# A two-layer megakernel: the last stores and last operand parts of three stages issued in the stage that follows

## The reference, cut to what matters

```python
x = L0_attn_in_features                      # [4, 1024, 128] f32
xn = _layernorm(x)
s = _L0_attn_ref(xn, ...)                    # RoPE, causal softmax attention, 16 heads of 8
g = _silu(_L0_ffn_ref(xn, ...))              # 128 -> 512 -> 128, gelu, with a low-rank term
x = x + s * g
xn = _layernorm(x)
s = _L1_attn_ref(xn, ...)                    # retention: qk * decay mask, / clip(sum|qk|, 1, 5e4), @ v, RMS norm, * silu gate
g = _silu(_L1_ffn_ref(xn, ...))              # mixture of 8 experts, top 2, capacity 614 of each
x = x + s * g
```

## Time and profile before

| | |
|---|---|
| three timed runs | 1003.27, 1003.89, 1009.45 us, median 1003.89 |
| the profiled execution | 1005.31 us |
| span of its instructions | 1003.5 us |
| mean granted TensorE clock | 0.936 of full speed |
| barrier into the attention | 118.7 us from the span's start |
| barrier into the layer change | 543.1 us |
| barrier into the retention | 651.1 us |
| barrier into the experts | 886.3 us |

### The profile page before, as it was taken

How to read it: one execution, slowest core, us unless ns; L and a number is a source line. 1 busy time by engine, 2 the same in 40 slices (tenths; PEclk the granted TensorE clock), 3 DMA queues, 4 the chain that set the end, 5 groups by cost and what they waited for, 6 DMA issues and landing times. The chain is left out here.

```text
span 1003.5 us, 25274 instructions
## 1 busy us (share of the span) xinstructions
PE 868.0 (86%) x9413; PEld 464.8 (46%) x9414; DVE 799.3 (80%) x1691; ACT 726.1 (72%) x1493; POOL 290.2 (29%) x331
## 2 busy tenths in 40 slices
PE   3999899999999999999898799788899999979960
PEld 3676544333433333333333677533444444458850
DVE  6665499999999999999831565289999999938895
ACT  2666408888888888888775455388999999948851
POOL 4875311111111000000003666600344443005560
PEclk9999859999999999999989789969999999979995
DMA  5579861644444354430005678597364542546637
GB/s 167 201 266 331 290 152 42 206 100 102 107 102 117 85 126 78 80 71 21 13 13 139 211 241 231 172 221 142 70 119 94 115 90 54 136 143 192 209 116 253
DMA packets 119385, 140.92 MB, mean 140 GB/s; under 512 B 20109, under 2 KB 82138, under 8 KB 118624
## 3 DMA queue, kind: packets, MB, share of 16 engines
q1 hardware_dynamic: 113888, 127.45, 46.6%
q0 software_dynamic: 5376, 11.85, 4.1%
HBM read 77.63 MB, written 63.25 MB: 140 GB/s over the span
## 5 line engine op out<-in xcount | busy, mean ns | idle before, releaser
L868 ACT ACTIVATE probsB<-psB 128x512 f32<-128x512 f32 (+2 forms) x640 | 310.2, 565 | 86.3 <-PE psB L942 59.3
L779 DVE TENSOR_REDUCE mxB<-psB 128x1 f32<-128x512 f32 (+2 forms) x448 | 256.9, 647 | 9.8 <-PE psB L906 8.3
L935 PE MATMUL psB<-q_groups,k_groups 64*128 64x512 bf16 (+3 forms) x768 | 206.4, 332 | 15.1 <-DVE mxB L779 8.3
L906 PE MATMUL psB<-k_groups,q_groups 64*128 64x512 bf16 (+3 forms) x768 | 216.9, 343 | 2.9 <-PEq L306 1.7
L973 PE MATMUL psB<-probsB,vB 128*32 128x512 f32 (+3 forms) x1536 | 165.3, 502 | 0.7 <-ACT probsB L868 0.5
L1751 ACT ACTIVATE psD<-psD 128x896 f32<-128x896 f32 (+2 forms) x192 | 153.4, 799 | 14.6 <-PE psD L1805 14.4
L935 PEld LDWEIGHTS psB<-q_groups,k_groups 64*128 64x128 bf16 x768 | 67.5, 94 | 160.4 <-ACT probsB L868 140.9
L1682 DVE TENSOR_REDUCE sumsD<-psD 128x1 f32<-128x128 f32 (+3 forms) x256 | 113.8, 487 | 13.2 <-PE psD L1828 11.0
L1805 PE MATMUL psD<-k_groups,q_groups 64*128 64x512 bf16 (+3 forms) x384 | 102.7, 341 | 17.6 <-PEq L1063 6.5
L913 PE MATMUL psB<-hideB,chooseB 64*128 64x128 bf16 (+1 forms) x1024 | 115.1, 210 | 0.0
L779 DVE TENSOR_REDUCE mx2B<-psB 128x1 f32<-128x384 f32 (+2 forms) x192 | 104.8, 598 | 8.5 <-PE psB L913 6.4
(11 more groups left out here) (226 smaller groups left out, 1495.0 us busy)
## 6 DMA issues: line engine op xcount, KB each, us to landing
v<-vaugA SPq DMA_DIRECT2D x4, 2048.0 KB, 8.9
vB<-v SPq DMA_DIRECT2D x16, 512.0 KB
q_groups<-q SPq DMA_DIRECT2D x32, 200.0 KB
k_groups<-k SPq DMA_DIRECT2D x32, 200.0 KB
back<-emptyB POOLq DMA_DIRECT2D x16, 256.0 KB, 3.8
o<-outB SPq DMA_DIRECT2D x128, 32.0 KB, 1.8
xD<-xn SPq DMA_DIRECT2D x8, 512.0 KB, 7.1
q<-hiA SPq DMA_DIRECT2D x12, 256.0 KB, 6.6
```

What stands on the lines that cost most here:

```text
L779: nc.vector.tensor_reduce(dst, src, AX.X, ALU.max).then_inc(max_read, 1)
L868: nc.scalar.activation(probs[:, n % DEEP, 0:w], st[n % BANKS][:, 0:w], ACT.Exp, scale=DH ** -0.5).then_inc(exp_done, 1)
L906: ins = nc.tensor.matmul(bank[:, to:to + w], q[half[r], s, hq // 2, t * P:t * P + P], k[half[r], s, hq // 2, HALF * c:HALF * c + w], start ...
L935: ins = nc.tensor.matmul(bank[:, to:to + w], k[half[r], s, hq // 2, jt * P:jt * P + P], q[half[r], s, hq // 2, i0:i0 + w], start=True, sto ...
```

## The change

`LastParts` and `LastBanks` are buffers that outlive one stage; `last_out` lies with the buffers of the layer change. At the three stage ends:

1. Attention to layer change: the 4 stores of the last half group (x = 15, c = 1) go to the start of the layer change on SP. ACT of the layer change no longer waits for them (`wait_heads_but_last`), SP still does, before it loads the last denominators.
2. Layer change to retention: of the last batch the `mid` stores (2 DMAs) and the `lo` part (4 POOL subtractions of 128x512 and 2 DMAs) go to the retention. There POOL forms `lo` with 2 subtractions of 128x1024 right at the start. SP issues the `mid` stores behind the 24 group loads, and the `lo` stores between the expert inputs of batches 1 and 2; batches 2 and 3 are loaded over the same memory, so SP waits there until all four stores have landed.
3. Retention to experts: the last group's `o` (4 DMAs) and `sums` stores and the last `diag` store go to the start of the expert stage on SP, ahead of its loads.

The labels of the expert rows are written by 8 POOL copies of 128x16 and not by 2 of 128x64. DVE and POOL get a wait for the stores of `project_and_ffn` in the attention, since other memory now lies under their buffers; the maxima `mx`, `mx2` move to `Groups`, and the final `x1` and `res` take the memory of `outD` and of `LastParts`.

```diff
+def store_heads(sp, A, x, c, held, stored):
+    b, s = divmod(x, QUADS)
+    for hq in range(4):
+        sp.dma_start(A["o0"][b, 4 * s + hq, :, c * HALF:(c + 1) * HALF], held[VW * hq:VW * hq + 2 * DH, :]).then_inc(stored[c], 16)
+class LastParts:
...
+    def form_lo(self, nc):
+        for j in range(2):
+            ins = nc.gpsimd.tensor_tensor(self.lo[:, j, :], self.rest[:, j, :], self.mid[:, j, :], ALU.subtract)
+        ins.then_inc(self.ready, 1)
+    def store(self, sp, A, name, part):
+        for layer, parts in (("q1", Q_PARTS), ("k1", K_PARTS)):
+            r, j = DH * parts[name], 0 if layer == "q1" else 1
+            sp.dma_start(A[layer][B - 1, :, r:r + DH, :], part[:, j, :]).then_inc(self.stored, 16)
...
+    def wait_heads_but_last(self, engine):
+        for c in range(2):
+            engine.wait_ge(self.heads_stored[c], HEAD_STORES * (B * QUADS - c))
...
             engine.wait_ge(self.x1_stored, 32 * B + 1)
         for i in range(2):
-            engine.wait_ge(self.second_stored[i], 16 * SECOND_STORES * (B // 2) + 1)
+            engine.wait_ge(self.second_stored[i], 16 * (SECOND_STORES * (B // 2) - 4 * i) + 1)
...
-                    store(x, 1)
+                    if x + 1 < NQ:
+                        store(x, 1)
...
                     if n == AHEAD:
+                        kept_until.wait_rows(dve)
...
+                kept_until.wait_rows(pool)
                 for x in range(NQ):
                     split_maxima(x)
...
+                store_heads(sp, A, B * QUADS - 1, 1, second.last_out, kept_until.heads_stored)
                 kept_until.wait_heads(sp)
...
-                        sp.wait_ge(g["mid_ready"], count[i]["mid_ready"])
-                        store_parts(i, "mid", mid)
-                        sp.wait_ge(g["lo_ready"], count[i]["lo_ready"])
-                        store_parts(i, "lo", lo)
+                        if not last or i == 0:
+                            sp.wait_ge(g["mid_ready"], count[i]["mid_ready"])
+                            store_parts(i, "mid", mid)
+                            sp.wait_ge(g["lo_ready"], count[i]["lo_ready"])
+                            store_parts(i, "lo", lo)
...
-                        for half, c in enumerate(halves):
+                        for half, c in enumerate(halves if not last or i == 0 else ()):
                             pool.wait_ge(g["mid_ready"], at(2, half + 1))
...
-                kept_until.wait_heads(act)
+                kept_until.wait_heads_but_last(act)
...
                 for s in range(GROUPS_AHEAD, QUADS):
                     groups.load_second(sp, A, 0, s)
+                last_parts.store(sp, A, "mid", last_parts.mid)
                 kept_until.wait_second(sp)
...
                 for b in range(B):
+                    if b == 2:
+                        sp.wait_ge(last_parts.ready, 1)
+                        last_parts.store(sp, A, "lo", last_parts.lo)
+                        sp.wait_ge(last_parts.stored, 64)
                     for kk in range(2):
-                        sp.dma_start(x[:, b, kk, :, 0:D], A["xn1"][b].rearrange("p (t c) -> p t c", c=D)).then_inc(x_loaded, 16)
-
-                for n in range(BANKS + 1):
+                        sp.dma_start(x[b][:, kk, :, 0:D], A["xn1"][b].rearrange("p (t c) -> p t c", c=D)).then_inc(x_loaded, 16)
+
+                for n in range(BANKS):
...
-                    if n % 4 == 3:
+                    if n % 4 == 3 and n + 1 < BANKS:
...
                 nc.gpsimd.memset(ones[:, :], 1.0).then_inc(cleared, 1)
+                last_parts.form_lo(nc)
...
+                last_banks.store_inside(sp, A, B * QUADS - 1, kept_until.inside_stored)
+                last_banks.store_sums(sp, A, B * QUADS - 1, kept_until.sums_stored)
+                last_banks.store_diagonal(sp, A, B * QUADS * NT // 2, kept_until.diag_stored)
                 load_retention(0, slice(0, 4))
```

More of the change, by code:

```diff
@@ L661, in attention @@
         empty = m.sb("emptyB", [P, SLOT_TILES, ROW])
-        out = m.sb("outB", [P, 2, HALF])
+        out = [m.sb("outB", [P, HALF]), second.last_out]
         v = m.sb("vB", [P, QUADS, NT, 4 * VW])
@@ L854, in keep @@
                         act.wait_ge(out_stored[c], STORED * x)
[L855 removed]
+                    nc.scalar.copy(out[c][:, :], pv).then_inc(out_kept, 1)
                 act.wait_ge(g2["in_loaded"], 16)
@@ L1027, in _, with between_layers @@
                     products(*y)
-def between_layers(nc, A, groups, L, second, order, kept_until):
+def between_layers(nc, A, groups, L, second, order, kept_until, last_parts):
     with Space(nc) as m:
@@ L1563, in routing, with __init__, store_inside, store_diagonal @@
     return exponentials, count_tokens, choose, index, weight, routed
-def retention(nc, A, groups, L, order, expert, kept_until):
+BANKS_KEPT = 8
+class LastBanks:
+    def __init__(self, m):
+        self.out, self.sums = m.sb("outD", [P, BANKS_KEPT, HALF]), m.sb("sumsD", [P, QUADS, 4 * (NT - 1)])
+    def store_inside(self, sp, A, g, stored):
+        b, s, first = g // QUADS, g % QUADS, 4 * (g % 2)
+        for hq in range(4):
+            sp.dma_start(A["o1"][b, 4 * s + hq].rearrange("r (j i) -> r j i", j=4),
+                         self.out[VW * hq:VW * hq + DH, first:first + 4, 0:2 * P]).then_inc(stored[g % 2], 16)
+    def store_diagonal(self, sp, A, n, stored):
+        group, pair = divmod(n - 1, 2)
+        b, s, c = group // (2 * QUADS), group // 2 % QUADS, group % 2
+        sp.dma_start(A["diag"][b, s, 4 * c:4 * c + 4, 2 * P * pair:2 * P * pair + 2 * P],
+                     self.out[0:P:VW, n % BANKS_KEPT, 2 * P:4 * P]).then_inc(stored[n // 4 % 2], 16)
+    def store_sums(self, sp, A, g, stored):
+        b, s = divmod(g, QUADS)
+        sp.dma_start(A["sums"][b, s], self.sums[:, s, :]).then_inc(stored[s], 16)
+    def rows(self):
+        return self.out[:, :, :].rearrange("p n f -> p (n f)").rearrange("p (b t c) -> p b t c", b=B, t=NT)
+def retention(nc, A, groups, L, order, expert, kept_until, last_parts, last_banks):
     SLOTS_D, PIECES = 12, 18
-    SCORE_RING, PIECE_RING, DEEP, DEEP_ABS, BANKS_KEPT = 2, 3, 8, 12, 8
+    SCORE_RING, PIECE_RING, DEEP, DEEP_ABS = 2, 3, 8, 12
     NQ = B * QUADS
@@ L1601, in retention @@
         counts = m.sb("countsD", [P, 2, HALF])
-        x, token = m.sb("xD", [P, B, 2, NT, ROW]), m.sb("tokenD", [P, B, 2 * NT])
-        out = m.sb("outD", [P, BANKS_KEPT, HALF])
+        x, token = [m.sb(f"xD{b}", [P, 2, NT, ROW]) for b in range(2)] + last_parts.rows(), m.sb("tokenD", [P, B, 2 * NT])
+        out, sums = last_banks.out, last_banks.sums
         absd = m.sb("absD", [P, DEEP_ABS, 4 * P])
@@ L2237, in program @@
         project_and_ffn(nc, A, groups, kept_until)
-        with Space(nc) as n:
-            second = SecondLayer(n, kept_until)
-            attention(nc, A, groups, second, kept_until)
-            between_layers(nc, A, groups, logits, second, order, kept_until)
-        expert = ExpertBuffers(m)
-        retention(nc, A, groups, logits, order, expert, kept_until)
-        experts_and_finish(nc, A, groups, expert, kept_until)
+        with Space(nc) as later:
+            last_parts = LastParts(later)
+            with Space(nc) as n:
+                second = SecondLayer(n, kept_until)
+                attention(nc, A, groups, second, kept_until)
+                between_layers(nc, A, groups, logits, second, order, kept_until, last_parts)
+            expert, last_banks = ExpertBuffers(later), LastBanks(later)
+            retention(nc, A, groups, logits, order, expert, kept_until, last_parts, last_banks)
+            experts_and_finish(nc, A, groups, expert, kept_until, last_parts, last_banks)
 def constants():
```

63 lines of the change are left out of this document (33 added, 30 removed).

## The result

| | before | changed |
|---|---|---|
| median of 20 runs each | 1007.38 us | 1001.0 us |
| ratio, 95% interval | | 0.9936 (0.992 to 0.9952) |
| profiled execution | 1005.31 us | 999.11 us |
| span | 1003.5 us | 997.3 us |

The gain is 6.4 us, by the interval 4.8 to 8.1. The forecast was 9.1. That is a change within 1%, as was held likeliest, and the time of 1001.0 lies 1.2 us above the range and 6.2 above the forecast of 994.8. Two things add up in that: a gain that is 2.7 us too small, and a base that was 3.5 us too low. The three runs shown of before had a median of 1003.89, its 20 runs have one of 1007.38. From there the same 9.1 us would have given 998.3.

A forecast was written before the change was run, and what follows sets the result against it. No engine fills the span; SP ends all three stages last and the others wait. Boundary gains 4.3 + 4.2, retention queue -0.2 and third boundary 0.8 sum to 9.1 us, so 1003.89 becomes 994.8 us; range 990.5 to 999.8.

The forecast's parts named there:

- First barrier: Attention to layer change: without SP's 4 last stores ACT drains last and the barrier comes 2.5 us earlier.
- First clock: Start of layer change: shorter PE pause keeps the clock up, first 8 matmuls take 3.60 us, not 5.37; 1.8 us saved.
- Layer change of 102.6 us: Sign in the changed profile: barrier into the retention comes 102.6 us behind the one into the layer change.
- Second boundary: Layer change to retention: 3.6 us earlier barrier, 1.5 less wait for v, 0.9 lost to POOL; 4.2 us gained.
- magnitude operation: Early retention: DVE's first operation on magnitudes is blocked until POOL's second subtraction ends, costing 0.9 us.
- wait at v: Early retention: PE's 1.84 us wait at its first product with v shrinks by 1.5 us, with fewer stores ahead.
- Retention's queue: Inside the retention: SP's first output stores go out 38 us behind the barrier; a small ACT stall costs 0.2 us.
- Third boundary: Retention to experts: barrier 3.4 us earlier, but PE waits 2.5 us for loads at `turn_sums`; 0.8 us gained.
- Rival (b): Clock falls at first boundary, third gives -0.7, v's wait stays: gain 4.3 us, 999.6 us; chance 0.23 including between.
- Rival (c): SP's late retention stores stall ACT, PE and DVE, then each us costs one; 1010 with 15 us stall; chance 0.04.
- The base: Time before, taken as 1003.89 us, the median of the runs shown, from which the gain was subtracted.

The follow-up runs named there:

- undo_first: Changed kernel with only the attention to layer change boundary put back as before; ratio 0.9971 to the kernel before.
- undo_second: Changed kernel with only the layer change to retention boundary put back as before; ratio 0.9981 to the kernel before.
- lo_later: Changed kernel with two batches' expert-stage loads around the six moved stores, and POOL forming `lo` only after 9 score pieces are read; ratio 0.9888 to before.
- late_stores: Changed kernel with SP also waiting for 38 score pieces to be read before loading expert inputs of batches 2 and 3; 1002.49 us, 0.9955 to before.
- undo_third: Changed kernel with only the retention to experts boundary put back as before; 999.88 us, ratio 0.9931 to the kernel before.
- fed_clock: Changed kernel with 16 identity transposes on PE ahead of its wait for batch 0's five expert-stage loads; ratio 0.9931 to the kernel before.

## Why the prediction was right and wrong

- **First barrier, 2.5 us: right.** ACT is last to drain, 0.2 us ahead of the barrier. The moved stores cost nothing.
- **First clock, 1.8 us: mis-sized.** The clock held and the 8 matmuls took 3.67 us, as foretold. "Taken whole" was wrong: 0.6 us went to the contention of DVE and POOL that the sum had priced for the second boundary and not here, though the earlier trace rows show the very pair. At the reciprocal 1.15 us are left. The boundary measured 3.5 us by undo_first, foretold 4.3.
- **Layer change of 102.6 us: right for the kernel, wrong for the profiled execution.** The five other kernels that have both the first and the second edit give 102.5 to 103.3 in six executions; the changed kernel's execution of 104.2 is the exception. Part of it is the clock: the stage's mean granted clock is 0.92 in the four executions of 102.5 to 102.7, and 0.90 in those of 103.2, 103.3 and 104.2.
- **Second boundary, 4.2 us: right in the sum, one term unproven.** 4.5 by undo_second. The magnitude operation rose by 0.8 us (0.9 foretold). The wait at v is 0.67 us in the changed kernel, but 0.40 to 2.00 in seven executions with the second edit, and 1.19 without it in undo_second: the 1.5 us taken back there, from one wait of 1.84, are not borne out as a fixed gain. The product itself comes 6.9 us behind the barrier before, 6.2 in undo_second and 5.0 to 6.5 in the eight executions with the edit. The Trainium skill, "SBUF — State Buffer", section "Who interferes with whom", names this one-input operation among those that can contend; undo_second and lo_later bear it out.
- **Retention's queue, -0.2: right.** The stores went out 34.8 us behind the barrier and not 38, since the queue emptied in 4.1 us; no stall here, and one of 0.18 us in lo_later.
- **Third boundary, +0.8: the step that failed.** The landing (11.2 us) and the wait (2.07 us for 2.5) were right. The branch taken behind them was not: the sum set nothing against the 0.8 us for the clock, and had the fall only as a bound, -0.7. In the profiled execution the clock fell behind the wait, and the 40 matmuls lost 6.26 - 4.73 = 1.53 us. It doesn't fall every time: it did in undo_first, and not in undo_second and late_stores, where PE waited 1.2 us. How often it falls in unprofiled runs, and so how much of the 1.5 us the median bears, isn't known. undo_third puts the edit at -0.5 us, the expert stages' and retentions' lengths at (234.2 - 230.2) - (121.7 - 118.6) = 0.9; neither is sharp enough to tell 0.8 from -0.7. The Trainium skill, "TensorE: Matmul & The Clock Gate", section "HAM oscillation — how this bites in real kernels", describes DMA waits of about 3 to 5 us between bursts of matmuls that throw the clock back each time. That left a wait of 2.5 us undecided, and the prediction gave it to a rival for want of a row. The changed kernel, fed_clock and undo_second are rows for it.
- **The sum.** The single edits measure 3.5 + 4.5 - 0.5 = 7.5 us, the whole 6.4, the single ones to within 3 us either way; 9.1 lies outside the whole's. Of the missing 2.7 us the rows show 0.6 at the first boundary and 1.5 at the third; the rest is within the error. Rival (b) came for one of its three parts, the third boundary. Rival (c) did not: its stall, made on purpose in late_stores, comes as described, but that each us of it costs a us isn't shown.
- **The base, 3.5 us: the larger part of the miss in the time.** A median of three runs was taken as the time before. Its own spread, 1003.27 to 1009.45, and the profiled execution at 1005.31 said that it could be a few us off. The range held no term for that. Of the 6.2 us between 994.8 and 1001.0, 3.5 are the base and 2.7 the gain; either alone would have left the time inside the range.

## What to carry to other kernels

A store that is moved behind a barrier still stands in a queue: ask which loads stood behind it, and put those ahead. That order of the same eleven DMAs, not the moved barrier, decided the third boundary. A wait for DMA that PE meets in the middle of its matmuls costs its length and can then cost slow matmuls behind it; cover it or fill it. And a single execution's stage lengths can differ by several us where the clock rises and falls, so an edit of one or two us is read from its own rows, not from stage totals.

## What was not expected of the hardware

- A pause of 2.07 us of PE, which ended 11 us behind a barrier, was followed by a granted clock of 0.57 for 4 us, and one of 4.73 us at the same place (undo_first) by slow matmuls too. Pauses of 1.18 and 1.21 us there (undo_second, late_stores), 0.96 us (first barrier) and 0.52 us (fed_clock) were not. With 16 idle transposes in the wait the clock stayed at 1.00, in the one execution that has them.
- The same code at the start of the retention got a mean clock from 0.73 to 0.85 over its first 70 us, and the stage, where its end has the third edit and no stall is added, was 235.7 us long at 0.73 and 230.2 to 230.9 at 0.83 to 0.85.
- A magnitude operation on integers with one input in SBUF is held until POOL's running subtraction ends: 0.42 us became 1.18, 1.24 (undo_first) and 0.84, according to how much of POOL's instruction was left.
